# Moving the edge test and the picks of the extra tiles from GpSimd to VectorE, and the setup into the first preparation, in a two-layer graph kernel

## The reference

```
# layer 0
a      = adj + I;  d = a.sum(axis=2) ** -0.5
x      = layernorm(x + (d_i * a * d_j) @ (x @ W0) + b0)
# layer 1, per pair of nodes (i, j)
pre    = x_j @ W1[:128] + x_i @ W1[128:] + b1
msg    = gelu(layernorm(pre) * g1 + be1)
agg_i  = sum_j msg_ij * adj_ij
upd    = layernorm(concat(x, agg) @ W2 + b2) * g2 + be2
out    = layernorm(x + upd)
```

## Time and profile before

| | |
|---|---|
| median of 3 runs | 3824.88 us (3823.39 to 3827.58) |
| the profiled execution | 3831.64 us, span 3829.9 us |
| mean granted TensorE clock | 0.956 |
| busy PE / ACT / DVE / POOL | 3241.6 / 3115.1 / 2903.9 / 2147.4 us |
| GpSimd, scatters (L508) | 740.9 us in 512 |
| GpSimd, gathers (L523, L524) | 360.5 and 362.7 us in 768 each |
| GpSimd, edge test (L473) | 253.4 us in 128 |
| VectorE, picks (L1063) and extra picks (L1059) | 846.8 us in 1536 and 71.3 us in 128 |

### The profile page before, as it was taken

The page is one execution under the profiler, slowest core; times in us unless marked ns, Lnnn a source line. Parts: engine busy times, 40 slices in busy tenths (PEclk is TensorE's granted clock), DMA queues, the critical chain, the costliest instruction groups (busy, mean ns, idle before and its releaser), DMA issues.

```text
span 3829.9 us, 87330 instructions
## 1 busy us (share of the span) xinstructions
PE 3241.6 (85%) x26504; PEld 2970.4 (78%) x26505; DVE 2903.9 (76%) x6547; ACT 3115.1 (81%) x8326; POOL 2147.4 (56%) x2628
## 2 busy tenths in 40 slices
PE   3688888888879888888888988888988888888887
PEld 2588787878768787877877878787878778878877
DVE  3578777777778777877877877777877777878787
ACT  2688888878879788987888978888987888878887
POOL 2556664556645566554666555666555666555652
PEclk9899999999989999999999999999999999999999
DMA  1333232232322323323223223323222323223321
GB/s 36 107 99 104 94 112 75 91 98 92 110 79 84 98 93 109 102 80 96 98 89 108 96 82 98 106 87 115 84 89 91 112 88 115 79 85 98 99 89 44
DMA packets 284244, 355.69 MB, mean 93 GB/s; under 512 B 28208, under 2 KB 242736, under 8 KB 283696
## 3 DMA queue, kind: packets, MB, share of 16 engines
q1 hardware_dynamic: 250928, 231.55, 20.6%
q0 software_dynamic: 32768, 117.47, 8.1%
HBM read 223.09 MB, written 125.83 MB: 91 GB/s over the span
## 4 chain that ended last, share of the span: by engine, by line
PE 47%; POOL 19%; DVE 12%; issue 10%; ACT 9%; DVEq 1%; DMA 0%; ACTq 0%; SPq 0%; POOLq 0%; PEldq 0%
PE agg_even_ps L1297 8%; POOL table L508 7%; PE z_even_ps L1338 7%; PE z_odd_ps L1338 7%; POOL edge L473 6%; PE agg_odd_ps L1297 6%; PE p_ps L1153 4%; DVE pick L1063 3%; DVE spread L1092 2%; POOL rank_extra L524 2%; DVE msg L1038 2%; PE z_even_ps L1334 2%; PE z_odd_ps L1334 2%; ACT root L651 2%; ACT tmp L706 2%
## 5 line engine op out<-in xcount | busy, mean ns | idle before, releaser
L706 ACT ACTIVATE tmp<-nbr,r_sb 128x128 f32<-128x128 f32 x4224 | 1318.5, 389 | 25.0
L1063 DVE SCALAR_TENSOR_TENSOR pick<-rank,root_p 128x512 f32<-128x512 bf16 (+3 forms) x1536 | 846.8, 581 | 102.0 <-PE z_odd_ps L1338 53.6
L508 POOL DMA_INDIRECT table<-stage,row_id x512 | 740.9, 1447 | 170.5 <-issue 149.6
L1092 DVE SCALAR_TENSOR_TENSOR spread<-nbr 128x512 f32<-128x512 bf16 (+3 forms) x1536 | 823.3, 563 | 6.7 <-PE agg_even_ps L1297 5.5
L523 POOL COPY root_extra<-root_p 128x32 f32<-128x32 f32 (+4 forms) x768 | 360.5, 469 | 622.7 <-ACT root_p L665 622.7
L691 ACT ACTIVATE msg<-msg 128x768 f32<-128x768 f32 x768 | 647.1, 843 | 39.9 <-issue 20.0
L1297 PE MATMUL agg_odd_ps<-spread,msg 128*128 128x128 f32 x4608 | 583.8, 277 | 26.7 <-issue 19.1
L1338 PEld LDWEIGHTS z_even_ps<-mi_g,pick 128*128 128x128 f32 x4608 | 572.2, 193 | 27.6 <-issue 3.3
L1338 PEld LDWEIGHTS z_odd_ps<-mi_g,pick 128*128 128x128 f32 x4608 | 571.1, 193 | 26.0 <-issue 0.7
L1038 DVE TENSOR_TENSOR msg<-z_odd_ps,tmp 128x768 f32<-128x768 f32 x384 | 364.2, 949 | 296.0 <-ACT tmp L706 294.1
L1338 PE MATMUL z_odd_ps<-mi_g,pick 128*128 128x129 f32 x4608 | 582.4, 276 | 0.0
(11 more groups left out here) (213 smaller groups left out, 4671.0 us busy)
## 6 DMA issues: line engine op xcount, KB each, us to landing
nbr<-table SPq DMA_DIRECT2D x128, 640.0 KB, 4.8
adj_g<-in_adj SPq DMA_DIRECT2D x32, 1024.0 KB, 6.7
nbr_root<-table SPq DMA_DIRECT2D x128, 256.0 KB, 5.8
nbr_extra<-table SPq DMA_DIRECT2D x384, 70.0 KB
nbr_extra<-table SPq DMA_DIRECT2D x128, 90.0 KB
nbr_extra<-table SPq DMA_DIRECT2D x256, 40.0 KB
x_g<-in_x SPq DMA_DIRECT2D x32, 256.0 KB, 3.1
table<-stage,row_id POOLq DMA_INDIRECT x512
```

The costliest lines, as they stand in the source:

```text
L508: pool.indirect_dma_start(table[q], bass.IndirectOffsetOnAxis(ap=row_id[:, jt * TB + it:jt * TB + it + 1], axis=0), stage[:, jt, it, :], N ...
L706: last = act.activation(tmp[:, c % 2, n - FROM[u], :], half_row, ACT.Identity, scale=r_sb[:, c % 2, n - FROM[u]:n - FROM[u] + 1])
L1063: ins = dve.scalar_tensor_tensor(into.rearrange("p k n -> p (k n)"), rank[:, it % 2, span], float(MARK + t), root_p[:, it % 2, span], ALU. ...
L1092: ins = dve.scalar_tensor_tensor(into, ranks(nbr[:, it, jt:jt + count, A_RANK:A_ROOT]), float(MARK + t), nbr[:, it, jt:jt + count, A_ADJ:A ...
```

## The change

GpSimd's `sort`, its edge test, the buffers `rank_extra` and `root_extra` and the semaphore `t_extra` go. VectorE tests the edges in step s = 2, two instructions in slot 1 and two in slot 3, after a wait for the degrees. The extra picks become 14 instructions on VectorE that read `rank` and `root_p` run by run, with the place number as an immediate. The setup on VectorE is cut in three, which run in the first graph's preparation ahead of s = 3 (weights), s = 8 (limits) and s = 12 (splits; `be1` is now split once and copied twice, where it was split three times). ScalarE waits only for the constants of GpSimd, TensorE for the weights ahead of the first product with `W0` (DMA alone), for the first part ahead of the ranks, and for the splits ahead of the first `mj`.

```diff
@@ gpsimd, prepare
-                if s == S_EDGE:
-
-                    wait_alone(pool, p_load, (a + 1) * 32)
-                    wait_alone(pool, p_deg, a + 1)
-                    for it in range(TB):
-                        last = pool.tensor_scalar(edge[:, it, :], adj_g[:, it, :], 0.0, 0.0, ALU.is_equal, ALU.is_equal)
-                    last.then_inc(p_edge, 1)
@@ gpsimd
-            def sort(n, k, t):
-                if t == T_EXTRA:
-                    wait_alone(pool, t_ev, n * NR + (R_ROOT + 1))
-                    if not is_int(n, 2):
-                        wait_alone(pool, c_pick, n * NM - NM)
-                    for at_piece, ((first, reps, stride, w), _) in zip(PIECE_AT, PIECES):
...
-                        pool.tensor_copy(root_extra[:, k % 2, span].rearrange("p (r n) -> p r n", n=w), columns(root_p[:, k % 2, :]))
-                        last = pool.tensor_tensor(rank_extra[:, k % 2, span].rearrange("p (r n) -> p r n", n=w), columns(rank[:, k % 2, :]),
-                                                  slots[:, span].rearrange("p (r n) -> p r n", n=w), ALU.subtract)
-                    last.then_inc(t_extra, 1)
@@ scalar
-            act.wait_ge(s_setup, 1)
+            act.wait_ge(s_ident, N_IDENT)
@@ vector, prepare
+                if s == S_EDGE and slot in (1, 3):
+                    if slot == 1:
+                        dve.wait_ge(p_load, (a + 1) * 32)
+                        dve.wait_ge(p_deg, a + 1)
+                    for it in (slot - 1, slot):
+                        last = dve.tensor_scalar(edge[:, it, :], adj_g[:, it, :], 0.0, None, ALU.not_equal)
+                    if slot == 3:
+                        last.then_inc(p_edge, 1)
@@ vector, steps
                         if jt == EXTRA:
-                            dve.wait_ge(t_extra, cx.tiles + (k + 1))
-                            ins = dve.scalar_tensor_tensor(into.rearrange("p k n -> p (k n)"), rank_extra[:, k % 2, :], 0.0, root_extra[:, k % 2, :],
-                                                           ALU.is_equal, ALU.mult)
+                            places_p = into.rearrange("p k n -> p (k n)")
+                            for at_piece, ((first, reps, stride, w), slot) in zip(PIECE_AT, PIECES):
+                                for rep in range(reps):
+                                    span = slice(first + rep * stride, first + rep * stride + w)
+                                    ins = dve.scalar_tensor_tensor(places_p[:, at_piece + rep * w:at_piece + (rep + 1) * w], rank[:, it % 2, span],
+                                                                   float(MARK + slot[rep]), root_p[:, it % 2, span], ALU.is_equal, ALU.mult)
@@ vector, alone
                 for s in range(GC):
+                    if s == S_X:
+                        setup_weights()
+                    if s == S_PRE:
+                        setup_limits()
+                    if s == S_HT:
+                        setup_splits()
@@ vector, setup_splits
-            for k in range(3):
-                split(be_split[0:3, k, 0:D], be1_all)
+                split(be_split[0:3, 0, 0:D], be1_all)
+                step(dve.tensor_copy(be_split[0:3, 1:3, :], be_split[0:3, 0:1, :].to_broadcast([3, 2, D + 1])))
+                dve.sem_inc(s_setup, 1)
@@ tensor
-            pe.wait_ge(s_setup, 1)
...
+                    if is_int(a, 1):
+                        pe.wait_ge(s_const, 16 * N_CONST)
...
+                            if is_int(a, 1):
+                                pe.wait_ge(s_setup, 1)
...
+                    if is_int(a, 1) and s == S_MJ:
+                        pe.wait_ge(s_setup, 2)
```

95 lines of the change are left out of this document (43 added, 52 removed).

## The result

The changed kernel took 3731.3 us (3730.02 to 3734.34), the kernel before 3826.23 us on the same chip: a ratio of 0.9752, 95% interval 0.9736 to 0.9769. That is 95 us faster, where the forecast was 248 us faster and the lower bound of the saving 145. The later runs add something that no forecast of mine had. They came in five sets, each with its own chip and its own runs of the kernel before, and in three of the sets the same changed kernel took 0.9507, 0.9479 and 0.9804 of the kernel before.

What follows compares the result with a forecast made beforehand. GpSimd's late `x_y`, stalling VectorE and then TensorE once per graph, was taken as the bound. Terms -180.8 - 55 - 21 + 31 - 22 = -248 us, from 3831.6 to 3583.6 (3577 as median); range 3480 to 3680.

Steps and rivals of the forecast that it cites:

- The stall: TensorE's wait for `sup`, once per graph behind GpSimd's late `x_y`, goes: -180.8 us.
- The cold product: The product with `sup` no longer runs at the slow clock after idling: 1.83 us times 30, -55 us.
- The table rows: Without gathers GpSimd's 16 scatters begin 2.3 us earlier, shortening TensorE's 43.0 us wait for `nbr`: half taken, -21 us.
- VectorE's new work: Fourteen picks (+3.6 us a graph) and edge test (1.35) moved to VectorE: +5.0 us a graph, mostly hidden.
- the 1.2 us a graph that might come back: Two VectorE picks beside the removed gathers took 2.10 us, 0.89 elsewhere; about 1.2 us might return.
- forecast +31 not hidden: Of VectorE's added work, 1.0 us a graph was taken to reach the end: +31 us.
- The setup: TensorE starts at 16.90 instead of 39.50 us, with some setup work still ahead of `x_v`: -22 us.
- C: Rival: scatters become the limit, each slowed 0.25 us by VectorE's denser instructions: +52 us, no -21, 3650 us; chance 0.06.
- A: Rival: VectorE's added work is not hidden, +156 us, no gain at the table rows: 3723 us; chance 0.16.
- D: Rival: short runs do not overlap, 11.8 us a graph, VectorE bounds at the tile boundary: 3920 us, slower; chance 0.04.
- E: Rival: `x_y` stays late because something else holds GpSimd; chance 0.02.

Runs made afterwards that it cites:

- e10: Changed kernel, with GpSimd's eleven other waits of a graph's first scatter put ahead of the wait for the first table-row quarter: 3558.56 us, ratio 0.9293.
- e8: e7, with TensorE turning the first row tile's ranks after `z` instead of before it: 3564.51 us, ratio 0.93.
- e12: Changed kernel with the edits of e8 (which include e7's) and e10 together: 3512.49 us, ratio 0.9174.
- e7: Changed kernel, with ScalarE writing the adjacency's last quarter to its own buffer, which GpSimd copies into `stage` later: 3632.47 us, ratio 0.9483.
- e9: The changed kernel unedited, run again on the third chip as base for e10 and e12: 3628.43 us, ratio 0.9479.
- e6: Changed kernel, with one pick of 384 (wrong) columns in place of the fourteen short picks: 3678.88 us, ratio 0.9593.
- e1: Kernel before with only the new setup; gathers, extra pick and edge test as before: 3738.74 us, ratio 0.9935.
- e5: The changed kernel unedited, run again on the second chip as base for e6, e7 and e8: 3639.41 us, ratio 0.9507.

## Why the prediction was wrong, by its own steps

**The stall, right.** -180.8 was forecast on TensorE, 176.7 went.

**The cold product, wrong.** The product did get warm, 1.78 us less, where 1.83 were forecast. But the step took the idle time ahead of TensorE to be gone, and it had moved: 2.15 and 2.78 us of new waits, after which `z` and `agg` took 2.79 + 2.26 instead of 2 x 1.50, 2.05 us more. Of the -55 nothing is left in the first trace, whose mean granted clock is 0.957, after 0.956 before. In e10, with a wait of 1.10 us in that place, the clock stayed up.

**The table rows, the step that failed.** "Without them the 16 scatters begin 2.3 us earlier", half of it taken, -21. (a) They begin 0.28 us earlier after their data (2.24 us instead of 2.52): of the 2.24, some 1.4 are eleven waits that GpSimd works off after the quarter is ready (e10). Before, 2.24 us after the quarter would have been 1707.46 and the gathers ended at 1707.57, so they hid them. I had taken the engine's last busy instruction for the cause; its own program, ahead of the scatter, had the answer. Moving the waits brought 70 us (e10). (b) The scatters' stretch got longer, 27.9 to 31.7 us, in the first trace; where it stayed at 29.3, the same kernel took 3639 and 3628 us. (c) A wait that I never counted hangs on them: ScalarE may not overwrite the last quarter of `stage` before the scatters of the graph before have landed, 15.5 to 113.6 us, and it passed 4.9 to 78.9 on to TensorE. Instead of gaining 21 us at this step, TensorE waited 41.7 (`nbr`) + 74.0 (`stage`) us more. That the path of the scatters bounds is shown by e8, e10 and e12, which shorten or take off waits on it and bring 68 us (against e7), 70 and 116 us (against e9). What the `stage` wait costs by itself is not shown; where graphs are short, taking it away brought next to nothing (e7).

Together: -176.7 + 41.7 + 74.0 - 22 = -83 us, the two halves of the clock about cancelling, against -95 measured.

**VectorE's new work, its size wrong and its effect too dear.** The edge test took 0.82 + 0.65 = 1.47 us (forecast 1.35). The fourteen runs cost what was forecast only where GpSimd was idle or scattering; by the mean they added 9.2 us a graph and not 3.6, because the sum had no term for what they cost beside GpSimd's own work (3.3 and 5.3 us). Other picks became cheaper, 846.8 to 779.1 us, which is the 1.2 us a graph that might come back, and more (2.1). VectorE's busy time rose by 6.6 us a graph. Yet of the forecast +31 not hidden nothing shows at the end (e6). That VectorE had room for this too is luck: the sum had asked for less.

**The setup, right.** TensorE starts at 16.40 us. The first `half` came 22.0 us earlier (89.91 before), e1 measured -24.

**The rivals.** C named the right place, the scatters, with 0.06 and a price of 0.25 us a scatter; measured were 0.22 us a scatter on the mean and 3.8 us a graph. That the size fits is in part luck: its reason, VectorE's denser instructions, is not borne out (e6), and with 29.3 us of stretch on other chips the price is 1.4. It lacked (a), (c) and the clock, and so gave 3650. The Trainium skill had more to say for it than I used: "DMA: Bandwidth & Descriptors", in its section on SWDGE, HWDGE and iDMA, says that the descriptor rings of a GpSimd DMA are SBUF state which GpSimd writes itself and from which VectorE locks it out in a 2-port mode. The traces agree that VectorE holds scatters up, 4.44 us for what takes 0.96 at its shortest, but none shows by which mode. A was refuted by e6. D's place was wrong, since the short runs do overlap (starts 0.08 us apart where GpSimd is not in the way), but its price of 11.8 us a graph was nearer to the measured 9.2 than mine; it took e6 to show that this does not reach the end. E was refuted by the waits.

The chance of faster, 0.94, came out. The range did not hold, since no case in it had the clock fall at another place or ScalarE's wait; the times of e5 and e9, 3639 and 3628, lie in it.

**Still open:** why the ninth scatter goes the long way in some graphs, with 0.91 to 0.92 us to the next `msg`, and the short way in others, with 0.92 to 0.94, mostly by chip but within one execution too (e5 and e8 have both kinds); and what stops TensorE on the chips where the kernel before takes 3764.

## What to carry to other kernels

When an engine's work is taken away, ask what its last busy instruction was hiding: waits that it works off one by one (0.13 us each here), and buffers that others may reuse only when its transfers have landed. Put the wait for the latest input last, and a read-back behind work that does not need it: these edits, with the buffer of e7, brought 116 us (e12 to e9), more than the change itself did on the first chip. Short instructions must be priced beside what the other engine does at that moment: fourteen of them took 1.37 us, and 5.3 beside GpSimd's copies. A gain of a few per cent belongs to the chip it was measured on until it is seen on another. A stall is only gone if nothing idles in its place for long enough to cost the clock again.

## What the runs showed of the hardware that was not expected

- A scatter's issue on GpSimd took 0.96 us at the shortest and up to 4.44 beside VectorE's instructions, with and without the change. Long and short graphs of one execution differ by 2.5 us on the mean; their scatters from the ninth on take 1.56, 1.43, 1.24 us and so on in one and 1.09, 0.96, 0.96 in the other (e5).
- Fourteen short picks on VectorE took 1.37 us from first start to next, and 5.3 us beside six instructions of GpSimd.
- One kernel ran at three speeds on four chips: 0.975 (all scatter stretches long), 0.948 to 0.951 (short) and 0.980 (short, but TensorE stops inside runs of matmuls). The kernel before took 3826 to 3829 us in four sets of runs and 3763 to 3764 in two.
- TensorE's `z` and `agg` ran at full speed after a wait of 1.10 us and slowly after 2.13 and 2.78.
